# LayerNorm scalars made one stage ahead for 24 of 32 batches, their root moved to GpSimd, fewer warm-up matmuls, and expert matmuls issued ahead of their weights, in an eight-stage decoder kernel

## What is computed

```
logits = tokens @ router_w.T + router_b          # F0: 8 experts, the best 2 taken
probs = softmax(logits);  top_p, top_i = top_k(probs, 2)
w = top_p / (sum(top_p) + 1e-10)
out = sum_k w_k * (x @ expert_weights[top_i_k])
out = out / max(sum(w), 1e-10) * (1 + sum(w) * 1e-10)
```

## Time and profile before

| | us |
|---|---|
| median of 3 runs (1717.78 to 1721.65) | 1719.74 |
| the profiled execution | 1722.42 |
| its span from first to last instruction | 1720.7 |
| stage starts in the span: A0, F0, A1, F1 | 15.0, 213.4, 307.7, 764.6 |
| A2, F2, A3, F3 | 905.0, 1125.9, 1404.9, 1594.2 |

### The profile page before, as it was taken

How to read it: one execution, slowest core, us unless ns; L and a number is a source line. 1 busy time by engine, 2 the same in 40 slices (tenths; PEclk the granted TensorE clock), 3 DMA queues, 4 the chain that set the end, 5 groups by cost and what they waited for, 6 DMA issues and landing times. The chain is left out here.

```text
span 1720.7 us, 45913 instructions
## 1 busy us (share of the span) xinstructions
PE 1569.8 (91%) x17355; PEld 1055.2 (61%) x17375; DVE 1059.8 (62%) x2291; ACT 932.8 (54%) x2341; POOL 560.2 (33%) x1017
## 2 busy tenths in 40 slices
PE   3998789899999999979996899979999987998898
PEld 2555454577777777766784556646777754554354
DVE  5677767566666666654346788862223235878676
ACT  3777536455565565544454566534333336775354
POOL 4565318233233233220202444200000005664772
PEclk8999899999999999989999899989999997999899
DMA  8544140000000000010105334010000026551000
GB/s 186 140 136 127 31 125 0 10 8 5 8 8 5 8 5 8 2 50 2 48 1 123 105 106 112 14 38 1 1 0 0 0 57 144 149 144 53 7 19 25
DMA packets 114003, 86.43 MB, mean 50 GB/s; under 512 B 19344, under 2 KB 110736, under 8 KB 113808
## 3 DMA queue, kind: packets, MB, share of 16 engines
q1 hardware_dynamic: 106592, 81.30, 17.3%
q10 hardware_dynamic: 7216, 2.45, 0.9%
HBM read 22.88 MB, written 2.10 MB: 15 GB/s over the span
## 5 line engine op out<-in xcount | busy, mean ns | idle before, releaser
L1105 DVE TENSOR_REDUCE neg_max<-scores 128x8 f32<-128x1024 f32 x192 | 226.7, 1181 | 75.2 <-PE scores L723 29.8
L2240 POOL TENSOR_TENSOR probs<-probs,inverse 128x512 f32<-128x512 f32 x128 | 133.0, 1039 | 314.6 <-DVE inverse L2445 314.6
L2379 ACT ACTIVATE probs<-scores,neg_max 128x128 f32<-128x128 f32 x512 | 180.7, 387 | 5.3 <-DVE neg_max L2437 5.3
L969 ACT ACTIVATE probs<-turned 128x1024 bf16<-128x1024 f32 (+1 forms) x128 | 131.1, 1024 | 84.5 <-PE turned L746 84.5
L1898 ACT ACTIVATE hidden_f<-hb_f,b_f 128x512 f32<-128x512 f32 x128 | 87.9, 687 | 128.9 <-PE hb_f L1844 128.7
L554 POOL TENSOR_TENSOR k_all<-k_all,k_parts 128x512 f32<-128x512 f32 x24 | 27.8, 1158 | 389.2 <-ACT k_parts L895 389.2
L2370 ACT ACTIVATE heads_t<-heads 128x512 f32<-128x512 f32 x64 | 38.2, 597 | 166.5 <-PE heads L2305 166.5
L1853 PEld LDWEIGHTS yb_f<-w_f,hidden_f 128*128 128x128 f32 x1024 | 119.2, 192 | 14.8 <-issue 14.8
L1853 PE MATMUL yb_f<-w_f,hidden_f 128*128 128x128 f32 x1024 | 119.3, 275 | 0.0
L1844 PE MATMUL hb_f<-xn_all_f,w_f 128*128 (+1 forms) x256 | 116.8, 600 | 0.0
L2379 ACT ACTIVATION_READ_ACCUMULATOR probs<-scores,neg_max 128x1 f32 x512 | 116.7, 228 | 0.0
(11 more groups left out here) (362 smaller groups left out, 3727.3 us busy)
## 6 DMA issues: line engine op xcount, KB each, us to landing
k_rep<-k_parts SPq DMA_DIRECT2D x144, 128.0 KB, 2.5
q_rep<-q_parts SPq DMA_DIRECT2D x129, 128.0 KB, 2.5
dense<-both SPq DMA_DIRECT2D x120, 64.0 KB, 2.1
ctx_t<-in_ctx_t_dram SPq DMA_DIRECT2D x24, 256.0 KB, 4.1
conv_weights_or_copies<-k_parts SPq DMA_DIRECT2D x32, 128.0 KB, 2.6
conv_weights_or_copies<-q_parts SPq DMA_DIRECT2D x32, 128.0 KB, 2.5
w_f<-in_L_ffn_W_dram SPq DMA_DIRECT2D x16, 256.0 KB, 3.1
x_state<-in_x_dram SPq DMA_DIRECT2D x4, 512.0 KB, 8.1
```

Of the source, the lines that this page charges most:

```text
L969: nc.scalar.activation(probs[:, b % 2, pair, :], turned[:, :], ACT.Exp, **bias).then_inc(s["exp_done"], 1)
L1105: v.tensor_reduce(neg_max[:, b % 2, 8 * pair + first:8 * pair + 8], scores[pair][:, first * S:].rearrange("p (h k) -> p h k", k=S), axis=X ...
L2240: nc.gpsimd.tensor_tensor(p4, p4, inverse[:, n % 2, CH * h:CH * h + CH].unsqueeze(2).to_broadcast([P, CH, S]), ALU.mult).then_inc(s["prob_ ...
L2379: last = nc.scalar.activation(probs[:, n % 2, h, c * S:(c + 1) * S], scores[n % 2][:, i * S:(i + 1) * S], ACT.Exp, bias=neg_max[:, n % 2, ...
```

## The change

1. A class `Norms` makes the scalars of a range of batches. In each stage up to A3 an instance `following` makes those of batches 0 to 23 for the next stage, once 24 batches have their statistics (`stat_done`, a semaphore that bn_stats now raises). In each stage after A0 an instance `late` makes those of batches 24 to 31 while the first ones are already in use. A0 keeps `norm_scalars`.
2. The root and reciprocal become one power of -0.5 on POOL, with two Newton steps on DVE behind it (`polish`, six instructions). ACT's Sqrt goes, and with it the table loads around it: ACT has 18 table loads before and 8 after.
3. keep_clock at stage heads: 10 to 3 in F0, F1 and F2, 8 to 3 in A1, 16 to 9 in F3.
4. F0: 6 keep_clock matmuls instead of 44, and PE then waits for `shifted` rather than for `weights_done` before the experts' matmuls; ACT and DVE still wait for the weights. The weights' formula is rearranged; the loops of DVE and POOL are unrolled. In F2 the router uses `choose` and `share`, as F1 did.

```diff
+class Norms:
+    def variances(self, dve):
+        v, mean, var, t = self.nc.vector, self.mean, self.var, self.tmp
+        self.link = link = Chain(dve, self.chain)
+        s6 = self.st.stats[:, self.first * 6:self.end * 6].rearrange("p (b s) -> p b s", s=6)
+        link(v.tensor_tensor(t, s6[:, :, 1], s6[:, :, 4], ALU.add))
+        yield
...
+        v.scalar_tensor_tensor(out=var, in0=t, scalar=0.25, in1=var, op0=ALU.mult, op1=ALU.add).then_inc(self.var_ready, 1)
+        yield
+    def root(self, pool):
+        pool.wait_ge(self.var_ready, 1)
+        self.nc.gpsimd.tensor_tensor(self.rstd, self.var, self.st.minus_half[:, :].to_broadcast([P, self.end - self.first]), ALU.pow) \
+            .then_inc(self.root_ready, 1)
+    def polish(self, dve):
+        v, link = self.nc.vector, self.link
+        dve.wait_ge(self.root_ready, 1)
+        for _ in range(2):
+            link(v.scalar_tensor_tensor(out=self.tmp, in0=self.var, scalar=-0.5, in1=self.rstd, op0=ALU.mult, op1=ALU.mult))
+            link(v.tensor_tensor(self.tmp, self.tmp, self.rstd, ALU.mult))
+            link(v.scalar_tensor_tensor(out=self.rstd, in0=self.tmp, scalar=1.5, in1=self.rstd, op0=ALU.add, op1=ALU.mult))
...
 # attention_small, POOL
+                if b == 6 and layer == 3:
+                    late.root(pool)
+                if b == (NB - 1 if select else NB + 1):
+                    following.root(pool)
...
 # attention_small, DVE
             normalise(0)
+            if select:
+                run(late_steps)
...
                     if c + 2 < NG:
                         normalise(c + 2)
+                    if c == 1:
+                        late.polish(dve)
                     if c < EARLY:
                         add_values(c)
...
+                    if layer == 3:
+                        run(late_steps, 1)
+                        if b == 8:
+                            late.polish(dve)
+                if b == NB - 2:
+                    dve.wait_ge(stat_done, READY)
+                    run(following.variances(dve))
+                if b == (NB if select else NB + 2):
+                    following.polish(dve)
...
 # linear_experts
-            pairs(pool, fold, NP)
+            late.root(pool)
+            for p in range(NP):
+                fold(p, p % 2, 0)
+                if p == NP - 2:
+                    following.root(pool)
...
-            keep_clock(nc, st, bank[7][:, :], 10)
+            keep_clock(nc, st, bank[7][:, :], 3)
...
-            keep_clock(nc, st, bank[7][:, :], 44)
-            pe.wait_ge(weights_done, 1)
+            keep_clock(nc, st, bank[7][:, :], 6)
+            pe.wait_ge(router.shifted, 1)
             for p in range(NP):
                 experts(p, p % 2)
...
-            pairs(dve, lambda p, r, half: feed.vector(dve, p, r, 0), NP)
+            for p in range(NP):
+                feed.vector(dve, p, p % 2, 0)
+                run(late_steps, 1)
+                if p == 9:
+                    late.polish(dve)
...
-            pairs(dve, add_experts, NP)
+            for p in range(NP):
+                add_experts(p, p % 2, 0)
+                if p == NP - 3:
+                    dve.wait_ge(stat_done, READY)
+                    run(following.variances(dve))
+            following.polish(dve)
             statistics(NP - 1)
```

More of the change, by code:

```diff
@@ L308, in norm_scalars, with __init__, run @@
     return on_vector, on_scalar
+READY = 24
+class Norms:
+    def __init__(self, nc, st, tag, first, end):
+        self.nc, self.st, self.first, self.end = nc, st, first, end
+        self.chain, self.var_ready, self.root_ready = (nc.alloc_semaphore(f"{n}_{tag}_{first}")
+                                                       for n in ("norms_chain", "norms_var", "norms_root"))
+        self.mean, self.rstd, self.var, self.tmp = (t[:, first:end] for t in (st.mean, st.rstd, st.ln_var, st.ln_tmp))
+    def variances(self, dve):
[4 more added lines that the diff above has]
+        yield
+        link(v.tensor_scalar(mean, t, 0.5, None, ALU.mult))
+        yield
+        link(v.tensor_tensor(t, s6[:, :, 1], s6[:, :, 4], ALU.subtract))
+        yield
+        link(v.tensor_tensor(t, t, t, ALU.mult))
+        yield
+        link(v.tensor_tensor(var, s6[:, :, 2], s6[:, :, 5], ALU.add))
+        yield
+        link(v.tensor_scalar(var, var, 1.0 / D, LN_EPS, ALU.mult, ALU.add))
+        yield
+        v.scalar_tensor_tensor(out=var, in0=t, scalar=0.25, in1=var, op0=ALU.mult, op1=ALU.add).then_inc(self.var_ready, 1)
+        yield
+    def root(self, pool):
[9 more added lines that the diff above has]
+            link(v.scalar_tensor_tensor(out=self.rstd, in0=self.tmp, scalar=1.5, in1=self.rstd, op0=ALU.add, op1=ALU.mult))
+def run(steps, n=7):
+    for _ in range(n):
+        next(steps, None)
 BIG = 2.0 ** 100
@@ L1905, in _ @@
         def _(dve):
-            ln_vector(dve)
+            late_steps = late.variances(dve)
             link = Chain(dve, chain)
             v = nc.vector
-            pairs(dve, lambda p, r, half: feed.vector(dve, p, r, 0), NP)
+            for p in range(NP):
+                feed.vector(dve, p, p % 2, 0)
+                run(late_steps, 1)
+                if p == 9:
+                    late.polish(dve)
             weights_vector(dve, link)
@@ L2021, in _ @@
                 first, end = groups[k]
+                if k == 4:
+                    late.root(pool)
                 pool.wait_ge(amax_done, k)
@@ L2157, in _ @@
                     residual(b - 1)
+                run(late_steps, 2)
+                if b == 8:
+                    late.polish(dve)
+                    dve.sem_inc(late_ready, 1)
                 for k in range(3, len(groups)):
@@ L2236, in _ @@
             for n in range(NO):
+                if n == 6:
+                    late.root(pool)
+                if n == NO - 3:
+                    following.root(pool)
                 for h in range(2):
@@ L2476, in _ @@
                 invert(n + 1, 0)
+                run(late_steps, 1)
+                if n == 9:
+                    late.polish(dve)
+                if n == NO - 6:
+                    dve.wait_ge(stat_done, READY)
+                    run(following.variances(dve))
+                if n == NO - 1:
+                    following.polish(dve)
 TOP_QUERIES = int(5.0 * np.log(250))
```

147 lines of the change are left out of this document (69 added, 78 removed).

## The result

| | before | after |
|---|---|---|
| median, us | 1719.14 (1717.78 to 1721.65, 4 runs) | 1740.55 (1736.04 to 1750.72, 4 runs) |
| ratio, 95% interval | 1 | 1.0134 (1.0108 to 1.0161) |
| span of the profiled execution | 1720.7 | 1749.0 |

What follows compares the result with a forecast made beforehand. TensorE's 91% busy priced nothing; what counts is what comes last at stage heads, F0's logits to experts, and tails. Heads -3.1, tails +3.7, F0 -7.6 gave -7.0, rounded -7.2: 1715.2 profiled, median 1712.5, range 1704 to 1720.5.

Steps and rivals of the forecast that it cites:

- part 1: Stage heads F0 to F3: scalars removed, fewer warm-up matmuls, -3.1 us in all; F0 -0.5 (first two pairs 2.75), F1 -1.2.
- the clock stays low: Rival: loops behind heads in F0, F1, F3 stay at 0.51 clock; one costs 7 us, total 1719.7; chance 0.10.
- a lower clock in the first 15 us of F0 or F1: Sign that the forecast is wrong: clock lower than before in the first 15 us of F0 or F1.
- part 3: The power on GpSimd: 1.1 us taken for 128x24, between bounds of 0.23 and 4.6, with issue 4.7.
- slow-power rival: Power takes 4.7 us and blocks POOL in A0, F0, A3, F1: 11.2 lost against 7.2 gained, 1723.7; chance 0.12.
- Its point of decision, 3.5 us: Power's time on POOL from which its loss outweighs the forecast gain: about 3.4 us up (7.2 / 3 + 1.1 = 3.5).
- 1.4 was forecast: A2's head: the late chain's polish ahead of the added values costs +1.4 us, part of A2's +1.9.
- 0.5 forecast, bound 1.5: A2's head: the pair mask's DMA beside the context may delay the keys, +0.5 us, between 0 and 1.5.
- the forecast -0.9: A1's head: context lands at 309.84, keys had started at 310.91; 1.0 less 0.1, so -0.9 us.
- -1.9: F3's head: nine warm-up matmuls instead of sixteen save at most 2.2 us; -1.9 taken.
- The 7.6: F0, `shifted` to last expert: weights in 9.45 us, early experts, PE gap 3 to 4.5; end 294.8 against 302.34, -7.6.
- the ten switches of the forecast: ACT's ten table loads removed: 0 taken; rival counting them in full, 1700, or 26.6 us and near 1686; chance 0.03.

Runs made afterwards that it cites:

- experiment 1: Changed kernel with the old counts of warm-up matmuls at stage heads (10 in F0, F1, F2, 8 in A1, 16 in F3): 1731.26 us, ratio 1.0049.
- experiment 4: Kernel before with only the fewer warm-up matmuls at stage heads (3 in F0, F1, F2 and A1, 9 in F3): 1746.09 us, ratio 1.0135.
- experiment 16: Changed kernel with six warm-up matmuls in F0, three in F1, no GpSimd power, A2's polish and mask later, A1's variance steps spread: 1724.22 us, ratio 1.0024.
- experiment 3: Changed kernel with two integer steps on DVE for the root's first guess instead of the power on GpSimd: 1730.24 us, ratio 1.0042.
- experiment 15: Changed kernel, power on GpSimd, with six warm-up matmuls in F0 and F1, A2's polish and mask later, A1's variance steps spread: 1725.42 us, ratio 1.0029.
- experiment 5: experiment 1 with A2's six polish steps moved behind the values and the fourth group's copy: 1728.56 us, ratio 1.0037.
- experiment 7: Changed kernel with ten warm-up matmuls in F0 and F1, DVE guess instead of power, A2's polish later, pair mask's DMA behind A2's first keys: 1713.18 us, ratio 0.9951.
- the later kernels: Kernels run after experiment 8, with the mask's DMA placed as in experiment 7; A2's keys start 2.9 to 3.7 us behind the context's issue.
- experiment 10: Changed kernel with old warm-up counts, no GpSimd power, A2's polish and mask later, A1's seven variance steps one to a loop step: 1717.11 us, ratio 0.9978.
- experiment 2: Changed kernel with F0's 44 warm-up matmuls and the wait for the weights again ahead of the experts: 1746.01 us, ratio 1.0130.
- experiment 8: Kernel before with only F0's experts started at `shifted` and 6 warm-up matmuls instead of 44, old weights' formula: 1719.05 us, ratio 0.9987.
- experiment 12: Changed kernel with old head counts, no GpSimd power, A2's polish and mask later, F0's 44 matmuls and experts behind the weights: 1718.29 us, ratio 0.9999.

## Why the prediction was wrong

**The failed step is in part 1, F0's and F1's heads.** It gave the cold start "2.75" us for two pairs and let the clock then rise as before, and the paragraph on the clock trusted, which showed it back within 3.5 us. That window is one of experts, long matmuls in a row. The loop behind a head consists of transposes and logits with 8 columns, and with three matmuls ahead it didn't get out of the low clock for 30 us, in any of nine profiled heads. The two pairs took about 2 us, less than allowed; all sixteen took 9 us more. The rival named "the clock stays low" had the mechanism and its place, F0 and F1; it priced one loop at 7 us, half of it at half speed (measured 9.0 and about 12, all of it), and counted one loop where two were hit. The prediction's own sign, a lower clock in the first 15 us of F0 or F1, came true. Experiments 1, 4 and 16 show the cause: the counts by themselves cost 24 us in the old kernel, and about 15 in the new one. These 15 and the 16 or so of the power (experiment 3) are gross; what the experts gained stands against them in the 21.4.

**The power in part 3 was mis-sized.** 4.17 us for 24 columns and 1.66 for 8 against 1.1 taken; the upper bound of 4.7 was nearly right, and "nearer the lower end" was a guess about an operation that no row showed. Part of its cost is as the slow-power rival said: F0's end +3.7, A0's tail +2. Experiment 15 puts its whole price, against no power at all, at 0.0074, 12.7 us; that rival had 11.2 beyond the 1.1. Its point of decision, 3.5 us, was passed. A3 may carry some of it: it is 194.9 long on average in the six traces with the power and 191.8 in the nine with the steps on DVE, though the two groups overlap. Here two integer steps on DVE, 0.25 and 0.21 us on 128x24, did the power's work ahead of the same Newton steps. The Trainium skill ("GPSIMD Engine Reference", 4.1 Engine selection) sends elementwise additions, multiplications and maxima to VectorE, with GpSimd about twice as slow on two inputs. The measurement is on that side, by a larger factor, though for an operation that the Trainium skill gives no price for in that row.

**A2 was half right.** The polish ahead of `add_values` was named as its loss; 1.4 was forecast, and the six steps took 945.58 - 942.67 = 2.9, as two of them ran beside POOL's work and took 1.01 and 1.07. PE then worked at the low clock: experiment 5 gives 3.8 back. The mask's DMA delayed the keys by 1.2 in experiment 7, and by 1.3 to 2.1 by the later kernels (0.5 forecast, bound 1.5); the context landed 4.8 us after its issue instead of 2.7.

**A1's loss was missed.** Its keys did start earlier, 2.3 us behind the first warm-up matmul instead of 3.2, the forecast -0.9. But with three matmuls ahead these keys ran at the low clock for part of the time and took 5.48 instead of 3.81, +1.7, which is the failed step once more. And the seven variance steps in one step of its loop cost 1.4 (experiment 10), a term that the prediction's sum did not have. Together +2.2, of +2.4 measured. Experiment 4, which has the counts but not the variance steps, lost 3.3 there.

**Right:** the weights (9.5 us, 9.45 forecast), the experts from `shifted` to the end (-7.7 against -7.6), the gap of 3.78 us (3 to 4.5), the earlier start of A1's keys. F3's -1.1 against -1.9 proves nothing: it varies from 122.1 to 125.6 between kernels with the new scalars. The 7.6 went on paper to the early experts and the formula together; alone, the early start is worth 2.8 to 3.4 in F0 (experiments 2, 8, 12), and nothing that the totals can tell.

**Table loads.** No experiment took them away alone. The traces have 19 of them before, not 18, and 8 after, so eleven went. The fastest kernels are without these eleven and about 8 us faster than before, of which F0 alone accounts for 6 to 7. By the Trainium skill ("ScalarE: Activation LUTs", What ACT_TABLE_LOAD costs) the ten switches of the forecast would be an estimated 26.6 us. It is hard to find room for that here. In the earlier trace rows the root waited for DVE's chain and not for the load beside it, so at that head the load's price on the path is near zero.

**Open** stays why A3 and F3 vary by several microseconds between kernels that are the same there (A3 from 189.5 to 195.8 without the power), and what part of experiment 15's loss is the clock. Open is also what decides at a head between the two outcomes of the last section: the count ahead moves it, but four and six matmuls gave both.

## What to carry to other kernels

A matmul whose result nobody reads may be what keeps the loop behind it at full clock: before it is cut, look at the granted clock in the stretch that follows, and price that whole stretch at the low level, not the first microseconds. A recovery seen in dense matmuls need not hold for a loop of short ones. An operation that the trace has never shown belongs beside idle time until it is measured, and small work moved into a serial engine's loop goes one step at a time, into the gaps.

## What the hardware showed unexpectedly

At the heads of F0 and F1 the clock had two outcomes and none between. In the 36 such heads of the eighteen profiled kernels, the low clock ended either 2.8 to 6.0 us after the stage's start or 30 to 34 us after it:

| warm-up matmuls ahead | early | late |
|---|---|---|
| 10 | 18 | 0 |
| 6 | 6 | 1 (F0 in experiment 15) |
| 4 | 1 (F1) | 1 (F0) |
| 3 | 0 | 9 |

F0's loop takes 1.60 us a pair at PE's 0.50 and 0.85 at 1.00, with PE 99% busy at the low level. A power on GpSimd takes 4.17 us for 128x24 and 1.66 for 128x8: 0.157 us for each further column and 0.4 fixed, where a plain operation on 128x16 takes 0.23. DVE steps on 128x8 that take 0.15 and 0.17 us alone took 1.07 and 1.01 while POOL worked beside them on tiles of 128x512, 1.15 us each.
